# Adapter 1 of a four-stage network: the residual sum moves from TensorE's accumulator to a VectorE instruction

## The reference

```
h = gelu(x @ W_down[role] + b_down[role])            # 256 -> 128
y = x + (h @ W_up[role] + b_up[role])                # 128 -> 256
out = (y - mean(y)) * rsqrt(var(y) + 1e-5) * gamma[role] + beta[role]
```

## Time and profile before

| | |
|---|---|
| median of 3 runs | 206.76 us (206.72 to 206.97) |
| the profiled execution | 206.47 us |
| its span, first to last instruction | 204.6 us |
| mean granted TensorE clock | 0.991 |
| busy: PE, DVE, ACT, POOL | 183.8, 119.0, 83.6, 44.1 us |

### The profile page before, as it was taken

The page is one execution under the profiler, slowest core; times in us unless marked ns, Lnnn a source line. Parts: engine busy times, 40 slices in busy tenths (PEclk is TensorE's granted clock), DMA queues, the critical chain, the costliest instruction groups (busy, mean ns, idle before and its releaser), DMA issues.

```text
span 204.6 us, 3299 instructions
## 1 busy us (share of the span) xinstructions
PE 183.8 (90%) x1101; PEld 160.0 (78%) x1101; DVE 119.0 (58%) x314; ACT 83.6 (41%) x178; POOL 44.1 (22%) x70
## 2 busy tenths in 40 slices
PE   0599998989999999999999999999999999998660
PEld 0567877888988888778888888899999999888440
DVE  2997687799668608981472621133556555556532
ACT  0452464554697406581244442035632454320140
POOL 8287366100000005000310000001124333114311
PEclk9999999999999999999999999999999999999996
DMA  4678679981503030230000000001023522032001
GB/s 108 212 216 245 212 238 271 258 256 21 191 0 106 2 103 0 103 106 0 0 0 0 3 0 0 0 0 46 10 84 112 161 84 82 0 105 74 29 0 53
DMA packets 18587, 17.85 MB, mean 87 GB/s; under 512 B 2049, under 2 KB 16970, under 8 KB 18570
## 3 DMA queue, kind: packets, MB, share of 16 engines
q1 hardware_dynamic: 16696, 14.59, 23.9%
q0 software_dynamic: 1024, 2.37, 4.1%
q10 hardware_dynamic: 850, 0.67, 1.0%
HBM read 16.58 MB, written 1.05 MB: 86 GB/s over the span
## 4 chain that ended last, share of the span: by engine, by line
PE 81%; DVE 9%; issue 3%; ACT 2%; DMA 2%; POOL 1%; DVEq 0%; ACTq 0%
PE bank L638 18%; PE bank L639 18%; PE bank L640 18%; PE bank L742 7%; PE bank L757 6%; PE bank L735 3%; PE bank L700 2%; PE bank L808 2%; DMA role_col_i<-in_itok_B 2%; PE bank L767 2%; PE bank L737 1%; PE bank L688 1%; DVE mw_l L1233 1%; DVE g_l L1385 1%; PE bank L797 1%
## 5 line engine op out<-in xcount | busy, mean ns | idle before, releaser
L1385 DVE TENSOR_TENSOR g_l<-g_full,g_h 128x512 fp32r<-128x512 f32 (+1 forms) x40 | 23.1, 585 | 33.2 <-ACT g_h L1020 32.9
L1017 ACT ACTIVATE g_full<-bank,vecs 128x512 f32<-128x512 f32 (+1 forms) x40 | 24.2, 605 | 41.5 <-PE bank L640 38.6
L1020 ACT ACTIVATE g_h<-bank,vecs 128x512 fp32r<-128x512 f32 (+1 forms) x40 | 24.0, 600 | 0.0
L1494 POOL TENSOR_TENSOR rstdA<-rstdA,power 128x1 f32<-128x1 f32 x16 | 9.5, 597 | 64.9 <-DVE rstdA L1241 64.9
L1521 POOL TENSOR_TENSOR x1T<-x1T,cms_full 128x512 f32<-128x512 f32 x4 | 6.0, 1498 | 57.8 <-DVE cms_full L1400 57.7
L638 PE MATMUL bank<-ao_h,mw_h 128*128 128x256 f32 (+1 forms) x48 | 16.7, 348 | 0.0
L638 PE MATMUL bank<-g_h,mw_h 128*128 128x256 f32 (+1 forms) x48 | 16.2, 338 | 0.0
L638 PE MATMUL bank<-cms_h,mw_h 128*128 128x256 f32 (+1 forms) x48 | 15.3, 318 | 0.0
L639 PE MATMUL bank<-cms_l,mw_h 128*128 128x256 f32 (+1 forms) x48 | 15.3, 318 | 0.0
L640 PE MATMUL bank<-cms_h,mw_l 128*128 128x256 f32 (+1 forms) x48 | 15.2, 318 | 0.0
L640 PE MATMUL bank<-g_h,mw_l 128*128 128x256 f32 (+1 forms) x48 | 15.2, 317 | 0.0
(11 more groups left out here) (251 smaller groups left out, 463.3 us busy)
## 6 DMA issues: line engine op xcount, KB each, us to landing
stage<-in_L_cond_mW SPq DMA_DIRECT2D x6, 512.0 KB, 3.4
stage<-in_L_cond_cW SPq DMA_DIRECT2D x4, 512.0 KB, 6.3
wdA<-in_L_cond_W_down SPq DMA_DIRECT2D x16, 128.0 KB, 2.5
wuA<-in_L_cond_W_up SPq DMA_DIRECT2D x16, 128.0 KB, 3.0
wdB<-in_L_cond_W_down SPq DMA_DIRECT2D x14, 128.0 KB, 2.5
wuB<-in_L_cond_W_up SPq DMA_DIRECT2D x14, 128.0 KB, 3.3
table_gamma<-in_L_cond_ln_w SPq DMA_DIRECT2D x1, 384.0 KB, 4.8
table_beta<-in_L_cond_ln_b SPq DMA_DIRECT2D x1, 384.0 KB, 6.5
```

The source lines that it names most:

```text
L1017: act.activation(g_full[n % 2][:, 0:width], bank[b][:, 0:width], ACT.Gelu, bias=bias)
L1020: act.activation(g[0][:, j, 0:width], bank[b][:, 0:width], ACT.Gelu, bias=bias).then_inc(g_high, 1)
L1385: dve.tensor_tensor(g[1][:, j, 0:width], g_full[n % 2][:, 0:width], g[0][:, j, 0:width].bitcast(F32), ALU.subtract).then_inc(g_ready, 1)
L1494: pool.tensor_tensor(var[:, k, 1:2], var[:, k, 0:1], power[:, :], ALU.pow).then_inc(done, 1)
```

## The change

In adapter 1 TensorE no longer turns x back into the accumulator. The bias product is the first write to the bank. After the up product VectorE adds the gathered rows `x_tok` to the accumulator and writes the sum to `yA`; statistics and centring then read `yA` instead of PSUM, and the centring writes in place. A new semaphore `sumA_ready` says that the sum is written: VectorE waits for it itself before the statistics, and it takes the place of `normA_ready` as what frees the PSUM bank. The wait for a free `yA` slot moves from the centring to the sum. Adapters 2 and 3 are not changed.

```diff
                 if layer == 0:
-                    take(b, normA_ready, place_of(0, c) + 1)
+                    take(b, sumA_ready, place_of(0, c) + 1)
...
-                for m in range(KD):
+                for m in range(KD if layer else 0):
                     pe.matmul(bank[b][:, m * P:(m + 1) * P], x[:, m, :], ident[:, :], start=(m == 0), stop=False,
                               is_transpose=True, skip_group_check=True)
-                pe.matmul(bank[b][:, 0:D], hot[:, c, :], bu[:, (0, 2, 3).index(layer), :], start=False, stop=True,
+                pe.matmul(bank[b][:, 0:D], hot[:, c, :], bu[:, (0, 2, 3).index(layer), :], start=(layer == 0), stop=True,
                           skip_group_check=True)
...
                     dve.wait_ge(upA_ps, i + 1)
+                    if layer == 0:
+                        if i >= YSLOTS:
+                            dve.wait_ge(normA_T_ps, i - YSLOTS + 1)
+                        dve.tensor_tensor(yA[k][:, :], x_tok[i][:, :], y, ALU.add).then_inc(sumA_ready, 1)
+                        dve.wait_ge(sumA_ready, i + 1)
+                        y = yA[k][:, :]
                     moments(y, statsA, mvA, rstdA, k, varA_ready)
...
                 dve.wait_ge(rstdA_ready, i + 1)
-                if i >= YSLOTS:
+                if layer == 0:
+                    y = yA[k][:, :]
+                else:
                     dve.wait_ge(normA_T_ps, i - YSLOTS + 1)
-                dve.tensor_scalar(yA[k][:, :], bank[chain_bank(layer, c)][:, 0:D], mvA[:, k, 0:1], rstdA[:, k, 1:2],
+                    y = bank[chain_bank(layer, c)][:, 0:D]
+                dve.tensor_scalar(yA[k][:, :], y, mvA[:, k, 0:1], rstdA[:, k, 1:2],
                                   ALU.subtract, ALU.mult).then_inc(normA_ready, 1)
```

More of the change, by code:

```diff
@@ L420, in build @@
         upA_ps = sem("upA_ps")
+        sumA_ready = sem("sumA_ready")
         varA_ready = sem("varA_ready")
```

## The result

| | before | changed |
|---|---|---|
| median | 206.74 us (206.23 to 206.97, 4) | 209.45 us (208.98 to 211.41, 4) |
| profiled execution, its span | 206.47, 204.6 us | 208.98, 207.1 us |
| its mean granted TensorE clock | 0.991 | 0.983 |

The ratio, taken over the single executions and so not the quotient of the two medians, is 1.0153 with a 95% interval of [1.0085, 1.0221]. A second comparison of the same two kernels, with 12 executions of the changed one, gave 208.69 against 206.74 us, 1.0076 [1.0044, 1.0109]. Both intervals lie above 1, so the change makes the kernel slower: by 1.8 to 4.6 us in the first comparison and by 0.9 to 2.3 us in the second. The forecast was 206.83, its range 206.1 to 207.5.

A forecast was written before the change was run, and what follows sets the result against it. TensorE set the pace up to 30 us, with VectorE just abreast and then on the path. Terms +0.02 - 0.22 - 0.19 + 0.46 - 0.13 + 0.13 = +0.07 us gave median 206.83, range 206.1 to 207.5.

The forecast's parts named there:

- From 15 to 31 us: Adapter 1 up to place 6's mask: VectorE's added work turns TensorE's gain into about 2.2 us of waiting; net +0.02 us.
- From 31 to 38 us: Place 6's `up` to `project`: shorter `down` and removed wait; `project` starts 0.02 - 0.22 - 0.19 = -0.39 us.
- The cover: Before place 5's turn: gathers end near 33.84, centring by 34.86, turn wants it at 34.98; hidden with 0.1 us to spare.
- the last power: POOL's power of place 7, held by the centring of place 6: 0.69 us long, 0.13 more; bounds 0 and 0.30.
- the rule on two-port modes: VectorE in a two-port mode and GpSimd exclude each other for a whole instruction; used to add 0.13 us at place 7's power.
- rival B: VectorE and POOL hold each other more often, at place 4's centring and place 7's power: +0.48 us, 207.24; chance 0.10.
- The last tile: Place 7 of adapter 1: unhidden sum +0.46 us, centring -0.13, POOL's power held +0.13.
- The clock: TensorE's granted clock was expected to stay 1.00 throughout, adding nothing to the time.
- Rival C: TensorE's clock falls in the new 2.2 us gap before place 6's `up`: +3 us, 209.8; chance 0.03.
- Rivals A: Adapter 1's centring gains nothing from SBUF, and the hold on POOL goes: +0.59 us, 207.35; chance 0.12.
- D: Adapter 1's instructions reading SBUF are shorter than assumed: centrings give 0.6 us in all, hence 206.2; chance 0.11.
- E: The sums find room on VectorE, TensorE's 1.5 us reaches place 6's mask: -1.5 + 0.4, about 205.6; chance 0.04.

The follow-up runs named there:

- Late gathers: POOL's four token-table gathers moved to the dense blocks: in the changed kernel 206.09 us, ratio 1.0016; in the kernel before 206.27 us, ratio 0.999.
- filled changed kernel: Changed kernel plus unused matmuls in TensorE's 1.44 us wait in adapter 2: 208.35 us with ten, 207.81 us with five.
- filled kernels: Unused matmuls in TensorE's 1.44 us adapter 2 wait, put into several versions; kernel before: 206.91 us with ten, 206.49 us with five.
- places 0 to 3: Kernel before with the change at its first four places only and token gathers moved to the dense blocks: 206.77 us; with five unused matmuls 205.23 us.
- the two kernels with more matmuls: Repeated matmuls added in the second dense phase: four in the kernel before, 206.78 us; eleven in the changed kernel, 211.6 us in two executions, 208.8 in two.

## Why the prediction was wrong

**Where the time went.** Of the 2.51 us between the two profiled executions, 1.14 are lost in adapter 1 and 1.36 by the clock at the end; 0.24 lie behind the last `yB`, and this execution's start-up was 0.23 shorter (14.22 - 13.99). The forecast had +0.07 for adapter 1 and nothing for the clock.

**"From 15 to 31 us"** held. Forecast: +0.02, the gap 2.2. Measured: -0.10, the gap 1.95. VectorE sets the pace, TensorE's 1.5 us become waiting. The price per tile was right: from the start of a sum to that of its statistics 0.45 us, where 0.46 was forecast, and 0.407 for the centring, where 0.41 was.

**"From 31 to 38 us"**, the start of `project`: -0.39 forecast, -0.76 measured. The removed wait gave back 0.44 and not the 0.19 that its row names. In the kernel before the matmul ahead of `project` is

```profile
33.34 0.38 PE L767 MATMUL bank<-ident,yA 128*128 128x128 f32 x2
```

and `project` follows 0.57 after its start (33.91); in the changed kernel it is 0.13 (32.79 and 32.92), because the two overlap. The split's cast takes 0.69 where it took 0.92: it meets a gather again, but this time the gather is the one held.

**"The cover" is the step that failed.** The forecast gave the way from `project` to the turn of place 5 no change (34.98 is again -0.39); measured it grew by 1.51 us, from -0.76 to +0.75. I had put the gathers' end at 33.84, by moving them as a block with the durations they had before, and found 0.1 us to spare. But VectorE's split moves as well, and the other way: 0.96 earlier (31.63 to 30.67; forecast 0.57), with the gathers 0.36 later (28.52 to 28.88; forecast 0.48). So they met anew. The second gather lost 0.34 and the third 0.70 us; they ended at 34.69, the power at 35.31, the centring began at 35.33 instead of 34.4, and TensorE waited 1.34 us. Most of that is the holds' 1.04 us; the gathers' later start is in it too. I had applied the rule to the last power, where the hold is 0.13, and never to the gathers, though the row at 33.38 says the same of anything on POOL begun inside the subtraction: it ends 0.42 after it, as if 0.42 of its undisturbed 0.55 us were still to do. Put to the gather at 31.78, the same arithmetic gives 32.61 plus 0.95 less 0.13, that is 33.43, which is when it ended. The forecast counted that row for the rule on two-port modes, but the instruction over it has two inputs and falls under the other rule of the Trainium skill, which is cited at the end of this text. It was rival B by kind, but B was priced at 0.24 and 0.17 by the nearest durations, not by a new layout of the two timelines. Its threshold of 0.33 was passed by the 1.04 us of the two holds. Late gathers remove the loss (tail -1.51), and a shift of the gathers alone brings a loss of the same kind to the kernel before (+0.56): both directions are shown.

**"The last tile"** held: from the turn of place 5 to that of place 7 the path grew by 0.45 us, +0.46 forecast, and the power of place 7 took 0.65 (0.69 forecast).

**The clock** was taken as unchanged, and that is the second term that failed: 1.36 us in the profiled execution. Rival C looked for the drop at the new gap; it came there too, in two profiles of the filled changed kernel, and cheaply. The dear one is at the end, where the change touches nothing. That it needs TensorE's sparse stretch there is shown by the filled kernels (0 of 24 against 16 of 127 for the kernel before, 0 of 24 against 10 of 12 for places 0 to 3). Why the same stretch takes 10 of 12 executions of one version and a few of the kernel before stays open: an alignment of that stretch with something outside the program would fit, but is not shown, and a shift alone, in the two kernels with more matmuls, didn't settle it.

Rivals A, D and E are excluded: the centring did gain, no instruction was shorter than forecast by 0.1 us per tile, and the sums found no free room. The forecast's chances of slower (0.27) and of B (0.10) were too low.

## What to carry to other kernels

When a change moves instructions on two engines that exclude each other, lay both timelines out anew, instruction by instruction, by the shifted starts; durations read before the change hold only for the overlaps of before. A margin of 0.1 us next to an operation whose length can go from 0.95 to 1.66 us is no margin. And where a kernel has a sparse stretch of TensorE ahead of its last dense work, check the granted clock there in several executions before believing a difference of 1%: filling the stretch is cheap as long as the fill fits inside the wait (0.05 us of tail for five matmuls, 0.56 for ten).

## What was not expected of the hardware

**A gather issued by POOL is held by a two-input VectorE instruction in SBUF.** Begun inside the subtraction (L1356, L1347) it takes 1.65 and 1.66 us, begun 0.24 ahead of it 1.02, alone 0.95 (rows above and the earlier trace rows). In all eight profiles where a gather begins inside that subtraction it takes 1.62 to 1.66 us. The Trainium skill ("SBUF — State Buffer", section "Who interferes with whom") says that a VectorE instruction with two SBUF inputs contends with a GpSimd one that reads SBUF, and that the order of issue decides who waits; these rows agree. The same section infers that such an instruction leaves the generation of descriptors alone. The rows show that the gather as a whole, which also reads its row numbers from SBUF, is nonetheless late by 0.7 us; which part of it is held was not tried.

**The cast holds and is held.** Begun 0.55 us into the gather at 31.08 it took 0.92 us instead of 0.69, and the gather its usual 0.95. Begun 0.49 and 0.36 us into the gathers at 30.18 and 30.74 it took 0.69, and the gathers ended 0.11 and 0.12 us after it. A gather with a first part that doesn't hold the cast and a later one that does would fit, with the border between 0.49 and 0.55 us; no run tried it by itself.

**Reading from PSUM costs VectorE nothing here, except in the centring.** Statistics take 427 ns from SBUF and 0.43 us from PSUM. Only the centring gains, 0.54 to 0.41 us, even with two scalars read per partition.

**The granted clock can fall after a gap of 1.95 us** in otherwise dense work (0.50 at 32 to 33 us) and needn't: it did in two of six profiles with that gap, and the first two profiles of the changed kernel show 1.00 there. The Trainium skill ("TensorE: Matmul & The Clock Gate", section "What's actually happening") says that the gate goes by how busy the array has been recently; the rows agree, and show that the same program can land on either side.
